# Three gathers a block in both layers of a graph network, and link tables made by masks and matmuls

## What is computed

```python
h = maximum(layernorm(x), 0)                       # per node, over 128 features
agg   = segment_sum(h[dst] @ Wn.T + bn, src, n)    # first layer: mean over the links
count = clip(segment_sum(1, src, n), 1, None)
x = x + h @ Ws.T + bs + agg / count
h = maximum(layernorm(x), 0)
deg  = segment_sum(1, dst, n); dis = deg ** -0.5   # second layer: symmetric norm
x = x + relu(segment_sum(h[src] * dis[src] * dis[dst], dst, n))
```

## Time and profile before

| | us |
|---|---|
| median of 3 runs (1206.85 to 1208.07) | 1207.74 |
| the profiled execution | 1204.19 |
| its span | 1202.2 |
| busy: TensorE / VectorE / ScalarE / GpSimd | 849 / 1036 / 1068 / 870 |
| mean granted TensorE clock | 0.789 |

### The profile page before, as it was taken

The page is one execution under the profiler, slowest core; times in us unless marked ns, Lnnn a source line. Parts: engine busy times, 40 slices in busy tenths (PEclk is TensorE's granted clock), DMA queues, the critical chain, the costliest instruction groups (busy, mean ns, idle before and its releaser), DMA issues.

```text
span 1202.2 us, 30432 instructions
## 1 busy us (share of the span) xinstructions
PE 849.3 (71%) x9310; PEld 783.0 (65%) x9408; DVE 1036.2 (86%) x2798; ACT 1067.9 (89%) x2780; POOL 869.7 (72%) x1133
## 2 busy tenths in 40 slices
PE   1589999999999999999899972444444444444444
PEld 1478999999989898888889861433333434334333
DVE  7899999989989989899988735888888888888886
ACT  2589999999999999999999945888888988889896
POOL 4777777777777777777777418777777777777771
PEclk9799999999999999999999995555555555555555
DMA  6346666666666666676666434888888889888894
GB/s 207 119 118 194 210 213 192 214 196 203 196 198 193 214 189 210 183 202 199 196 211 189 147 132 165 257 268 277 259 277 267 262 275 266 274 274 261 264 277 184
DMA packets 82230, 259.38 MB, mean 216 GB/s; under 512 B 19986, under 2 KB 20356, under 8 KB 82116
## 3 DMA queue, kind: packets, MB, share of 16 engines
q1 hardware_dynamic: 58948, 210.86, 55.4%
q0 software_dynamic: 22400, 46.91, 14.1%
q10 hardware_dynamic: 768, 0.20, 0.1%
HBM read 152.93 MB, written 104.37 MB: 214 GB/s over the span
## 4 chain that ended last, share of the span: by engine, by line
POOL 37%; issue 23%; ACT 19%; PE 7%; DVE 7%; DMA 4%; POOLq 2%; ACTq 0%; DVEq 0%
POOL X L694 30%; ACT work L804 11%; DMA X<-in_x,IDX 3%; ACT area L814 3%; ACT area L819 3%; PE p_O L984 2%; PE p_O L996 2%; POOL work L647 2%; POOL work L631 2%; POOL work L651 2%; PE p_T L959 1%; DVE ST L1419 1%; DVE area L1481 1%; ACT sd L776 1%; POOL factor L667 1%
## 5 line engine op out<-in xcount | busy, mean ns | idle before, releaser
L804 ACT ACTIVATE work<-X,shift,scale 128x128 f32<-128x128 f32 x1329 | 550.2, 518 | 2.0 <-DVE shift L1456 1.8
L694 POOL DMA_INDIRECT X<-in_x,IDX x392 | 389.2, 993 | 130.4 <-issue 97.3
L1419 DVE BATCH_NORM_STATS2 ST<-X 128x6 f32<-128x256 f32 x1176 | 409.4, 415 | 39.0 <-DMA X<-in_x,IDX 36.9
L1047 PE MATMUL p_O<-work 32*128 32x128 f32 x1984 | 205.4, 435 | 222.3 <-POOL work L635 138.8
L694 POOL DMA_INDIRECT X<-x_table,IDX x294 | 286.5, 975 | 93.2 <-issue 91.1
L1047 PEld LDWEIGHTS p_O<-work 32*128 32x128 f32 x1984 | 178.0, 323 | 242.8 <-issue 188.1
L804 ACT ACTIVATE p_O<-X,shift,scale 128x128 f32<-128x128 f32 x496 | 201.2, 444 | 25.4 <-DVE area L1503 23.1
L984 PE MATMUL p_O<-wnT,area 128*128 128x128 f32 x1568 | 217.6, 282 | 4.6 <-DVE area L1481 4.4
L996 PEld LDWEIGHTS p_O<-wsT,area 128*128 128x128 f32 x1568 | 206.8, 192 | 7.4
L996 PE MATMUL p_O<-wsT,area 128*128 128x128 f32 x1568 | 207.5, 275 | 5.2
L984 PEld LDWEIGHTS p_O<-wnT,area 128*128 128x128 f32 x1568 | 191.5, 192 | 7.3 <-DVE area L1481 7.2
(11 more groups left out here) (175 smaller groups left out, 1114.7 us busy)
## 6 DMA issues: line engine op xcount, KB each, us to landing
x_table<-area SPq DMA_DIRECT2D x98, 528.0 KB
X<-x_table SPq DMA_DIRECT2D x98, 528.0 KB
X<-in_x SPq DMA_DIRECT2D x98, 512.0 KB, 4.3
out_x<-area SPq DMA_DIRECT2D x98, 512.0 KB, 5.8
X<-in_x,IDX POOLq DMA_INDIRECT x392
X<-x_table,IDX POOLq DMA_INDIRECT x294
moved<-held SPq DMA_DIRECT2D x32, 12.2 KB
es<-in_src SPq DMA_DIRECT2D x1, 488.5 KB, 3.6
```

What stands on the lines that cost most here:

```text
L694: nc.gpsimd.indirect_dma_start(got(s)[:, k, 0:w], None, table, bass.IndirectOffsetOnAxis(ap=IDX[:, s, k:k + 1], axis=0)).then_inc(gathered ...
L804: last = nc.scalar.activation(o, row(l, s, r), ACT.Relu, bias=shift[:, s, r:r + 1], scale=scale[:, s, r:r + 1])
L1047: ends[half] = nc.tensor.matmul(outs1[p][g][:, c], SEL[1][q, p, part_of, :], H[1][q, p, draw, :], start=False, stop=(half == 1 and part_of ...
L1419: last = V.bn_stats(ST[:, s, r:r + 2, :].rearrange("p r k -> p (r k)"), pair.rearrange("p r c -> p c r"))
```

## The change

Layer one gets the tables of layer two: three gathers a block, 11 rows, and the sums in four row groups on four banks.

- The constants: `PAIRS`, `ROWS1` and `BANKS` go; `QUADS` = `PARTS` = 4, `ROWS` = `BT + DRAWS` = 11 for both layers. `hold_links`, `move_links`, `join_links` and the DMAs of ScalarE go.
- The codes are not doubled and transposed but spread over 128 columns under a mask (`of_quad`) in four parts and multiplied by a second mask (`of_block`) in four matmuls (`turn_lot`); ScalarE takes the result in one copy (`take_lot`). The same is done for the seven lots of link factors in steps 81 to 88, in place of the transposes behind layer one. There are 14 lots in all; all use one buffer `codes4`. A lot is turned after the sums of its step, and `decode` has three parts instead of two.
- `p_T` is one tensor of four banks, each with two transposed tiles; the counts and the small products lie in the fourth bank and are copied by ScalarE with the sums. The reciprocal of the counts reads that copy, and waits for it.
- The products have four banks, two per parity of the block: a neighbour product waits for the addition of the same half two blocks before.
- The last pair of statistics has one real row, which is read twice.

```diff
+        def out0(off, g):
-            return p_O[(2 * off + g) % BANKS]
+            return p_O[2 * (off % 2) + g]
...
+            def turn_lot(m):
+                pe.wait_ge(s_codes, m + 1)
+                if m > 0:
+                    pe.wait_ge(s_coded, m)
+                for k in range(PARTS):
+                    to = k if m < TB else min(k, DRAWS - 1)
+                    last = nc.tensor.matmul(scratch[:, to, :], codes4[:, k, :], of_block[:, :], start=(to == k),
+                                            stop=(m < TB or k != DRAWS - 1), skip_group_check=True)
+                last.then_inc(s_codeT, 1)
...
             def aggregate(turn, off):
-                if not first(i, 1):
-                    pe.wait_ge(counts_read, i)
-                for j in range(GT):
-                    for g in range(2):
-                        q = slice(SLOTS * g, SLOTS * g + SLOTS)
-                        nc.tensor.matmul(p_T[g][:, P * j:P * j + P], H[0][q, p, BT + j, :], SEL[0][q, p, j, :],
-                                         start=False, stop=(j == GT - 1), skip_group_check=True)
+                for k in range(DRAWS):
+                    for q in range(QUADS):
+                        of = slice(HALF * q, HALF * q + HALF)
+                        c = slice(P * k, P * k + P) if k < DRAWS - 1 else slice(0, 2 * P)
+                        part_of = SEL[0][of, p, k, :] if k < DRAWS - 1 else SEL[0][of, p, k:PARTS, :].rearrange("p a n -> p (a n)")
+                        nc.tensor.matmul(p_T[:, q, c], H[0][of, p, BT + k, :], part_of, start=False,
+                                         stop=(k == DRAWS - 1), skip_group_check=True)
+                if lot_at(off) is not None:
+                    turn_lot(lot_at(off))
...
             def neighbours(turn, off, g):
-                back, used = divmod(g + 1, 2)
-                if not first(i, 3 - back):
-                    pe.wait_ge(prod_used[used], i - 2 + back)
+                if not first(i, 2):
+                    pe.wait_ge(prod_used[g], i - 1)
...
+            def spread(m, values):
+                if m > 0:
+                    dve.wait_ge(s_codeT, m)
+                for k in range(PARTS):
+                    of = (slice(0, HALF), slice(0, HALF), slice(HALF, SLOTS), slice(SLOTS - 1, HALF - 1, -1))[k]
+                    c = slice(QUADS * (k % 2), QUADS * (k % 2) + QUADS)
+                    last = V.scalar_tensor_tensor(
+                        codes4[:, k, :].rearrange("p (q n) -> p q n", q=QUADS),
+                        values[:, of].rearrange("p (a n) -> p a n", a=1).to_broadcast([TP, QUADS, HALF]), 0.0,
+                        of_quad[:, c].rearrange("p (q a) -> p q a", a=1).to_broadcast([TP, QUADS, HALF]), ALU.max, ALU.mult)
+                last.then_inc(s_codes, 1)
...
             def inverse_counts(turn, off):
-                dve.wait_ge(aT_ps, i + 1)
+                dve.wait_ge(aT_sb, 2 * i + 2)
-                V.reciprocal(rc[:, off % HT, :], p_c[:, 0:BT]).then_inc(counts_read, 1)
+                V.reciprocal(rc[:, off % HT, :], summed(off, 1)[:, 1, 2 * P:2 * P + BT]).then_inc(counts_read, 1)
...
+    RUNS_AT, DIS_AT = 74, 81
...
+        if DIS_AT < k <= DIS_AT + TB:
+            return TB + k - DIS_AT - 1
...
             def beside(k):
+                if DIS_AT <= k < DIS_AT + TB:
+                    spread(TB + k - DIS_AT, roots[:, k - DIS_AT, :])
```

More of the change, by code:

```diff
@@ L44 @@
 HT = 5
-BANKS = 5
 LOT = (5, 4)
@@ L174, in group_of, with lot_at, tiles, of_half @@
         return min(i, NB - 1) // GROUP_BLOCKS
[L176 to L186, removed]
+    def lot_at(k):
+        if k == 2:
+            return 1
+        if DIS_AT < k <= DIS_AT + TB:
+            return TB + k - DIS_AT - 1
+        return next((g for g in BEGIN if BEGIN[g] + 11 == k), None)
+    def tiles(g):
+        return [(a, k, 2 * g + a + QUADS * k) for a in range(2) for k in range(2)]
+    def of_half(v, g):
+        return v.rearrange("p (k c) d -> p c k d", k=2)[:, 2 * g:2 * g + 2, :, :]
     def either(eng, fast, general):
@@ L931, in transpose_h @@
                     pe.wait_ge(aT_sb, 2 * i + g - 1)
-                for j in range(GT):
-                    last = nc.tensor.matmul(p_T[g][:, P * j:P * j + P], H[0][:, off % HR[0], GT * g + j, :], ident[:, :],
-                                            start=(j == 0), stop=False, is_transpose=True, skip_group_check=True)
+                if g == 1 and lot_at(off - 1) is not None:
+                    pe.wait_ge(s_coded, lot_at(off - 1) + 1)
+                if g == 1 and off - 1 == SUM_AT:
+                    pe.wait_ge(s_total_read, 1)
+                for a, k, j in tiles(g):
+                    last = nc.tensor.matmul(p_T[:, 2 * g + a, P * k:P * k + P], H[0][:, off % HR[0], j, :], ident[:, :],
+                                            start=(k == 0), stop=False, is_transpose=True, skip_group_check=True)
                 last.then_inc(hT_ps, 1)
@@ L961, in aggregate @@
-                if joins is not None:
-                    pe.wait_ge(s_coded, joins + 1)
-                if off == SUM_AT:
-                    pe.wait_ge(s_total_read, 1)
-                for j in range(PAIRS):
-                    c = 2 * j
-                    nc.tensor.matmul(p_c[:, c:c + 2], SEL_high[:, p, j, :, 1], halves[:, :], start=(j == 0), stop=False,
+                    nc.tensor.matmul(totals, ones[:, 0:1], checks[:, :, :].rearrange("p a b -> p (a b)"),
+                                     start=True, stop=True, skip_group_check=True).then_inc(s_total, 1)
@@ L1057, in fast @@
             def fast():
-                pe.wait_ge(s_disl, 1)
-                nc.tensor.matmul(p_O[1][:, :], ones3[:, :], bias3[:, :], start=True, stop=True)
-                nc.tensor.matmul(p_c[:, :], ones3[:, :], bias3[:, :], start=True, stop=True).then_inc(s_disT, 1)
+                pe.wait_ge(s_coded, 2 * TB)
+                for q in range(QUADS):
+                    last = nc.tensor.matmul(p_T[:, q, :], ones3[:, :], bias3[:, :], start=True, stop=True)
+                last.then_inc(s_open, 1)
                 schedule(1, pe, step1)
@@ L1403, in _ @@
             V.memset(verdict[0:1, 2, 1:2], float(loops))
[L1404 to L1406 removed]
+            done(V.memset(quarters[:, :], 0.0))
+            for q in range(QUADS):
+                last = V.memset(quarters[HALF * q:HALF * q + HALF, q:q + 1], 1.0)
+            done(last)
             split_bias()
```

372 lines of the change are left out of this document (143 added, 229 removed).

## The result

The changed kernel takes 1229.63 us (median of four runs, 1227.49 to 1232.84) against 1207.9 for the kernel before, now of four runs: a ratio of 1.018, 95% interval 1.016 to 1.0207. It is slower by 21.7 us; 9.7 slower was forecast. The profiled execution took 1229.6 us with a span of 1227.8 (before 1204.19 and 1202.2), at a mean granted clock of 0.778 (before 0.789).

A forecast was written before the change was run, and what follows sets the result against it. GpSimd's gather issue was taken to bound layer one after its head start, ScalarE before. Changes of +7.0 (blocks 6 to 97), +3.5 (start) and -0.8 (joint) gave +9.7, or 1213.9 profiled and 1217.4 us median; range 1193 to 1236.

The forecast's parts named there:

- the lots: Blocks 6 to 97: four small fp32 matmuls (eight records) per lot, twelve lots, 0.4 us each, +4.8 us.
- the clock in the stalls: Steps 82 to 87: TensorE's idle gaps pull the granted clock down each time, 6 x 1.6 = +9.8 us.
- the start: Start-up, VectorE one chain: more spreading, matmul records, decoding operations and counts by the copy, +3.5 us (2 to 5).
- the reciprocal: Layer one: VectorE's reciprocal of 448 columns, 2.89 us, no longer vanishes in VectorE's lag, +2.0 us.
- 91 plain steps: Block 6 to 97: TensorE sets each step at 6.28 us, 571.5 us in all, 33.8 less than before.
- six stalls, the wait: Steps 82 to 87: VectorE's single-buffer wait delays its addition and TensorE's neighbour products, 3.57 us six times, +21.4.
- decoding with marks, draws with spreading: Blocks 6 to 97: decoding meets first marks (0.5 over, four times), a draw meets spreading (0.1, five times), +2.5 us.
- its neighbours, other short ones: Blocks 6 to 97: 0.3 us for the neighbours of the 448-column reciprocal.
- joint, tail, layer two: Behind layer one: TensorE's seven transposes go, -0.8 us; layer two keeps its time.
- the rival of instruction-bound row groups: Sums over links: if 68 ns a record is a floor, +0.5 us a step, +42, or 1260 us; chance 0.06.
- the quicker TensorE: Plain steps 0.15 us shorter over 85 steps, 12.8 less, but VectorE stops it at about 1207 us; chance 0.08.
- The longer bank ring: Steps with a draw exceed 6.28 by 0.15 to 0.4 us, +10 to +25, or 1227 to 1242; chance 0.11.

The follow-up runs named there:

- the fourth gather: One unused indirect DMA more per layer-one block, against the kernel with two spread-code buffers and half 1's addition moved ahead (1190.28 us): 1208.05 us, ratio 1.0046.
- the extra row: ScalarE normalises row 0 of every block twice, against the kernel with two spread-code buffers and half 1's addition moved ahead (1190.28 us): 1200.42 us, ratio 0.9971.
- Two buffers: The changed kernel with two buffers for the spread codes, used in turn, nothing else different: 1191.88 us, ratio 0.989 to the kernel before.
- the early addition: The changed kernel, one buffer kept, with VectorE's addition of half 1 moved directly behind the reciprocal of the counts: 1210.05 us, ratio 1.0038 to the kernel before.
- The kernel with the filler: The changed kernel with 22 unread TensorE products in each of steps 83 to 88, to fill idle time: 1224.08 us, ratio 1.0159 to the kernel before.

## Why the prediction was right and wrong

The direction and the mechanism held; the size was too small by 12 us of the median, 1217.4 against 1229.63, and by 15.9 of the spans (25.6 against 9.7). The steps of the prediction that failed are prices, all of them too low: the lots (4.8, measured 10.8, the largest miss), the clock in the stalls (9.8, measured 14.2), the start with the step from block 6 to 7 (3.5, measured 6.7) and the reciprocal (2.0, measured 3.6). By the terms of its own sum:

| term | predicted | measured |
|---|---|---|
| 91 plain steps | 571.5 | 571.5 |
| six stalls, the wait | 21.4 | 21.6 |
| six stalls, the clock | 9.8 | 14.2 |
| twelve lots | 4.8 | 10.8 |
| decoding with marks, draws with spreading | 2.5 | 2.8 |
| the long reciprocal | 2.0 | 3.6 |
| its neighbours, other short ones | 0.3 | 0.9 |
| step from block 6 to 7 | in the start | 1.6 |
| sum, block 6 to 97 | 612.3 | 627.0 |
| start, up to block 6 | +3.5 | +5.1 |
| joint, tail, layer two | -0.8 | -1.2 |

- **Plain steps: right.** Neither the rival of instruction-bound row groups nor that of the quicker TensorE occurred: 24 records in 1.09 us. At the 114 ns that a record of a lot takes (below), 24 would have taken 2.7 us; layer two's rows, by which the prediction went, were the better guide. That the gain of 33.8 us has two sources, GpSimd and ScalarE, is shown by the fourth gather (17.8) and by the extra row (10.1), each added back alone. GpSimd's 6.7 us a block were added up loosely: 4 x 1.25 and 1.4 to 1.6 are 6.4 to 6.6, and the rest is 16.4 us of idleness behind L651 in the same row. The longer bank ring did not come: steps with a draw are 6.28. Only with the draw or the decoding meeting the spreading does the ring show, by 0.2 and 0.45.
- **The stalls: right in place and price.** 3.57 us each was forecast, 3.6 measured. The ring itself was 0.5 short, 10.25 where 10.8 came, for the lot in it; the step without the wait was short by the same 0.5 (6.68, measured 7.18), so the difference held. Two buffers remove it all, which settles the cause. VectorE was to wait "about 4 us" and waits 4.6 in the first stall and up to 6.4 in the last, longer where the clock was low; that idle time was not what set the step. Steps "of 10 to 12 us" came as 12.15 to 13.59.
- **The clock: right in kind, too small.** What failed is "6 x 1.6": the price was read from one fall of about three us. In the first stall the clock was low for as long and cost 1.4; in the other five it was low for nearly seven us each (from before 649 to 655.4 in the windows above), a part of it while TensorE idled, and cost 2.1, 2.5, 2.7, 2.8 and 2.8. The Trainium skill, page "TensorE: Matmul & The Clock Gate", section "HAM oscillation — how this bites in real kernels", says that a loop with a long wait for DMA in each turn throttles the array again in each. The six steps of the kernel after agree, though they wait for VectorE (3.45 us). With shorter pieces it was not every gap: the clock held in the last four steps of the early addition (about 2.5 us idle) and in three of the six filled ones (1.18).
- **The lots: the largest miss, 6.0 us.** "28 to 60 ns a record" was argued from the few columns that move. The lot takes 645.95 - 645.04 = 0.91 us for eight records, 114 ns each, and turning it twice adds 0.89. The Trainium skill, page "TensorE: Matmul & The Clock Gate", section "LDWEIGHTS (loading the stationary operand)", says that a load costs by the columns of the stationary operand, here 128: 107 ns by its figure. The lots' trace is near it, 114. Other rows are not: the 24 records of the sums take 45 ns each, and the four bf16 products of the counts, with as many stationary columns, 646.05 - 645.95 = 0.10 us together. No run changed the stationary columns, so that it is the load which costs 114 ns is likely and not shown. The prediction weighed this rule for the sums, where it didn't bind, and not for the lots.
- **The reciprocal: 3.6 and not 2.0.** Its own wait is 1.80 us; the clock then fell once more, which the sum had only for the six stalls. With the early addition the wait is 1.51, the clock holds and the step is 8.06:

```profile
572.94 1.59 PE L946 MATMUL p_O<-wnT,area 128*128 128x128 f32 x8 [1.80 <-DVE area L1419]
```

```profile
574.00:575.00 1.00, 1.00 (x6) 0.85 (x6) 0.75 (x3) 0.00 (x0) 0.79 (x2) 0.50 0.97 193
```

- **The start: 5.1 + 1.6 and not 3.5.** The first spreading, 0.90 us, stands for three short operations; the first lot's eight records took 1.89 us, behind 16.90 us without work, where those at 645.04 took 1.06, though the granted clock stands at 1.00 for both; and the decoding takes 29.28 - 27.11 = 2.17 us. After, with TensorE in it, then before, VectorE alone:

```profile
23.91 0.90 DVE L1153 SCALAR_TENSOR_TENSOR codes<-codes,of_quad 112x128 f32<-112x128 f32 x4
...
24.86 1.89 PE L864 MATMUL p_T<-of_block,codes 112*128 112x14 f32 x8 [16.90 <-DVE codes L1153]
...
27.11 0.19 DVE L1164 TENSOR_SCALAR decoded<-codeT 128x56 int32<-128x56 int32 x1 [1.72 <-ACT codeT L726]
...
29.28 0.65 DVE L1112 TENSOR_SCALAR X<-ed 128x977 int32<-128x977 int32 x1
```

```profile
24.97 0.19 DVE L1206 TENSOR_SCALAR decoded<-codeT 128x56 int32<-128x56 int32 x1 [0.60 <-ACT codeT L759]
...
26.41 0.64 DVE L1158 TENSOR_SCALAR X<-ed 128x977 int32<-128x977 int32 x1
```

  The decoding began at 24.97 and took 1.44 before. It now begins 2.14 later and takes 0.73 more; the first block's sums come 3.06 later, so these 2.9 are nearly all of it. The other 3.6 us are lost between blocks 0 and 7. Of these 1.1 are a fall of the clock. The kernel with the filler is the same up to block 82, and its step from block 4 to 5 is 9.92 and not 11.52, the next one 6.85 and not 6.28. Windows there, of the kernel after and of that one:

```profile
92.00:95.00 3.00, 3.00 (x15) 2.85 (x15) 3.00 (x10) 1.65 (x6) 1.60 (x2) 0.54 0.22 64
```

```profile
92.00:95.00 3.00, 3.00 (x45) 2.51 (x44) 3.00 (x9) 1.72 (x5) 1.04 (x2) 1.00 0.32 61
```

  Its first sums come 0.55 earlier too and its block 6 at 100.28, 3.5 later than before; so a part of the start differs from one execution to the next. For the rest TensorE waits for additions, as in

```profile
81.88 1.16 PE L946 MATMUL p_O<-wnT,area 128*128 128x128 f32 x8 [1.11 <-DVE area L1419]
```

  but which of the bank ring and the counts by way of the copy takes how much was not tried. The early addition did not help there: block 6 comes at 101.7 to 103.5 in the six kernels that have it, at 100.3 to 101.9 in the three changed ones that have not.
- **Joint, tail and layer two: right.** So was the claim that the masking, the 32 small DMAs and the joining had been hidden: the steps from block 73 on are the plain 6.28 and their neighbours.

The range held the time because it reached to 1236 for a clock cost of up to twice the estimate and for the longer ring. The ring was not needed; the clock took 4.4 us of that room, and the lots took 6.0, for which it allowed 3. So it is in part luck that the range held.

## What to carry to other kernels

A staging buffer between two engines that run at different points of the step needed two places here: the wait on it stalled not the transfer alone but everything queued behind, above all the addition that frees TensorE's banks. Price such a wait by its ring, look for the other rings behind it before moving an operation past it, and add for TensorE what the clock takes in the work after the gap. Don't price small fp32 matmuls by the columns that they move: with 14 of them a record of a lot took 114 ns here.

## What the runs showed of the hardware

- Eight fp32 records with 14 moving columns took 0.91 us, 114 ns each, with 128 stationary columns; 24 records in four row groups of 32 took 1.09 us, 45 ns each, the same as 16 records in two groups of 64. Four bf16 records with 4 moving and 128 stationary columns took 0.10 us.
- The granted clock did not go by the length of the idle piece alone. It fell to 0.50 with 3.45 us idle in all seven stalls (six of the kernel after, one unfilled), with about 2.5 us in two of six, with 1.80 in three of three steps with the reciprocal, with 1.3 to 1.5 in none of five such steps, and with 1.18 in three of the six filled ones. And it fell for three us in four steps in which TensorE was never idle, behind 16 small records of a doubled lot; behind the eight of a plain lot without idleness it never did.
- One fall cost 1.4 us (first stall of the kernel after, about three us low) to 2.8 (its last, nearly seven us low).
